# Last feed-forward stage: DMA transposes, two PSUM accumulator sets, a padded bias product and five steps in place of six

## The reference

```python
x = x + 0.5 * ffn(layernorm(x), weight, bias)
x = x + attention(layernorm(x), ...)
x = x + 0.5 * ffn(layernorm(x), weight, bias)      # the last stage

def ffn(x, weight, bias):
    # blocks of 32 channels: scale = max(|block|) / 7.5, values to the nearest of the FP6 grid
    xq, xs = mx_quantize(x)
    wq, ws = mx_quantize(weight)
    return (xq * xs) @ (wq * ws).T + bias
```

## Time and profile before

| what | value |
|---|---|
| median of 3 runs | 3375.26 us (3371.84 to 3376.33) |
| profiled execution: time | 3373.88 us |
| profiled execution: span of the trace | 3372.0 us |
| start of the last stage (its first load) | 2865.46 us |
| busy share over the span: PE, DVE, ACT, POOL | 89%, 68%, 56%, 57% |

### The profile page before, as it was taken

How to read it: one execution, slowest core, us unless ns; L and a number is a source line. 1 busy time by engine, 2 the same in 40 slices (tenths; PEclk the granted TensorE clock), 3 DMA queues, 4 the chain that set the end, 5 groups by cost and what they waited for, 6 DMA issues and landing times. The chain is left out here.

```text
span 3372.0 us, 68516 instructions
## 1 busy us (share of the span) xinstructions
PE 3001.5 (89%) x24864; PEld 1829.5 (54%) x24864; DVE 2306.3 (68%) x3170; ACT 1888.3 (56%) x2323; POOL 1911.1 (57%) x1497
## 2 busy tenths in 40 slices
PE   0399999999999999999978999999999999499999
PEld 0244444444444444444447877777777776244444
DVE  7467666666666766666556666666666665799995
ACT  2355555555555555556545666665666666566662
POOL 3354554554455455445326666666666665788883
PEclk9699999999999999999978999999999999699999
DMA  2123233323323323332247767677767674344442
GB/s 76 63 88 113 88 113 113 107 93 115 119 92 113 113 94 106 113 113 95 93 127 187 191 189 191 189 185 194 188 181 194 187 192 117 115 151 149 149 148 86
DMA packets 339610, 449.44 MB, mean 133 GB/s; under 512 B 23048, under 2 KB 254496, under 8 KB 331168
## 3 DMA queue, kind: packets, MB, share of 16 engines
q1 hardware_dynamic: 339360, 445.57, 43.4%
HBM read 243.85 MB, written 201.38 MB: 132 GB/s over the span
## 5 line engine op out<-in xcount | busy, mean ns | idle before, releaser
L761 DVE TENSOR_TENSOR fq_out_lo<-fq_val,fq_out_hi 128x512 f16<-128x512 f32 x384 | 460.7, 1237 | 289.8 <-ACT fq_out_hi L829 289.8
L946 PE MATMUL fq_acc<-fq_y_hi_t,w_qkv 128*128 128x512 f16 x2048 | 614.6, 379 | 1.6 <-ACT fq_y_hi_t L842 1.6
L1186 ACT ACTIVATE att_ctx<-att_o_ps 32x512 f32<-32x512 f32 x512 | 300.9, 588 | 365.0 <-PE att_o_ps L1295 358.7
L829 ACT CAST fq_out_hi<-fq_val 128x512 f16<-128x512 f32 x384 | 237.3, 618 | 319.1 <-DVE fq_val L758 311.0
L1270 PE MATMUL att_s_ps<-att_k,att_q_bd 128*128 128x44 f16 x6144 | 388.4, 217 | 26.2 <-DMA att_q_bd<-q_parts 16.9
L1270 PEld LDWEIGHTS att_s_ps<-att_k,att_q_bd 128*128 128x128 f16 x6144 | 382.1, 170 | 27.0 <-issue 26.0
L946 PE MATMUL fq_acc<-fq_y_lo_t,w_qkv 128*128 128x512 f16 x1024 | 388.5, 379 | 0.0
L946 PEld LDWEIGHTS fq_acc<-fq_y_hi_t,w_qkv 128*128 128x128 f16 x2048 | 200.1, 98 | 243.6 <-ACT fq_y_hi_t L842 1.8
L946 PE MATMUL fq_acc<-w_qkv,fq_y_hi_t 128*128 128x512 f16 x1024 | 304.9, 380 | 16.7 <-ACT fq_val L824 16.7
L966 PE MATMUL fq_acc<-w_ffn,fq_f_hi_t 128*128 128x512 f16 x1024 | 310.7, 386 | 1.4 <-DVE fq_f_lo_t L806 1.4
L632 PE MATMUL ffn_acc<-w_ffn,ffn_hi_t 128*128 128x512 f16 x1024 | 306.8, 381 | 4.5 <-DVE ffn_x_ring L518 4.4
(11 more groups left out here) (188 smaller groups left out, 6510.2 us busy)
## 6 DMA issues: line engine op xcount, KB each, us to landing
att_v<-v_parts SPq DMA_DIRECT2D x96, 704.0 KB
att_k<-k_parts SPq DMA_DIRECT2D x64, 524.0 KB, 7.1
fq_x<-in_L_attn_x SPq DMA_DIRECT2D x32, 1024.0 KB, 6.8
x_after_ffn<-fq_x SPq DMA_DIRECT2D x32, 1024.0 KB, 4.3
att_q_bd<-q_parts SPq DMA_DIRECT2D x512, 64.0 KB, 3.8
att_x<-x_after_ffn SPq DMA_DIRECT2D x32, 1024.0 KB, 5.9
x_after_attention<-att_x SPq DMA_DIRECT2D x32, 1024.0 KB, 9.2
ffn_x_ring<-x_after_attention SPq DMA_DIRECT2D x32, 1024.0 KB, 6.3
```

The costliest lines, as they stand in the source:

```text
L761: dve.tensor_tensor(out=out[1][:, b], in0=val[:, b % RING], in1=out[0][:, b], op=ALU.subtract).then_inc(s["out_lo"], 1)
L829: act.copy(out[0][:, b], val[:, b % RING]).then_inc(s["out_hi"], 1)
L946: op = pe.matmul(acc[:, b % RING], w, m, start=(kc == 0 and (a, c) == (0, 0)), stop=(kc == KC - 1 and (a, c) == PARTS[-1]))
L1186: return act.activation(ctx_f[rows, u.u % 2].rearrange("p g (c q) -> p g c q", q=CHUNK), o_ps[rows, :, :, h, :], ACT.Copy, scale=1.0 / P_UP)
```

## The change

The diff, cut to what acts. `LAG_*` are the distances of the pipeline's steps.

```diff
-    k.bias_ffn = keep("bias_ffn", [3, C], BF16)
+    k.bias_ffn = keep("bias_ffn", [P, C], BF16)
-    k.ones = keep("ones", [3, P], BF16)
+    k.ones = keep("ones", [P, P], BF16)
...
+                pool.memset(k.bias_ffn[:], 0.0).then_inc(bias_zero, 1)
...
-    LAG_LN, LAG_Q, LAG_LO, LAG_T, LAG_MM, LAG_OUT = range(1, 7)
+    LAG_LN, LAG_Q, LAG_LO, LAG_MM, LAG_OUT = range(1, 6)
...
-        acc = ctx.enter_context(nc.psum_tensor(tag + "acc", [P, SUB, C], F32))
+        acc = ctx.enter_context(nc.psum_tensor(tag + "acc", [P, 2, SUB, C], F32))
...
+                def turn(u, part, part_t, ready, done):
+                    if u.within(GROUPS):
+                        need(sp, s[ready], u.n + 1)
+                        take(sp, s)
+                        need(sp, s["multiplied"], (u.n - 1) * SUB)
+                        take(sp, s)
+                        sp.dma_start_transpose(part_t[:, u.u].rearrange("p i g n -> p (i g) n"),
+                                               part[:, u.u]).then_inc(done[u.u], 16)
...
                         sp.dma_start(dst_v[:, bass.ds(u.n, 1), :], xr[:, slot(u)]).then_inc(stored[u.u], 16)
+                    turn(t.back(LAG_LO), lo, lo_t, "lo_done", lo_turned)
+                    turn(t.back(LAG_Q), hi, hi_t, "hi_done", hi_turned)
...
-                        dve.tensor_scalar(scale[:, u.u], am[:, u.u], 1.0 / FP6_MAX, 1e-30, ALU.mult,
-                                          ALU.max).then_inc(s["floored"], 1)
-                        need(dve, s["floored"], u.n + 1)
-                        dve.tensor_scalar(scale_up[:, u.u], scale[:, u.u], LN_UP * FP8_UP, None, ALU.mult)
-                        dve.reciprocal(rscale[:, u.u], scale[:, u.u]).then_inc(s["scales"], 1)
-                    u = t.back(LAG_T)
-                    if u.within(GROUPS):
-                        need(dve, s["turned_lo"], u.n + 1)
-                        need(dve, s["multiplied"], (u.n - 1) * SUB)
-                        dve.tensor_copy(lo_t[:, u.u], t_lo[:]).then_inc(s["lo_out"], 1)
+                        dve.tensor_scalar(scale_up[:, u.u], am[:, u.u], SCALE_UP / FP6_MAX, SCALE_UP * 1e-30, ALU.mult,
+                                          ALU.max).then_inc(s["floored"], 1)
+                        need(dve, s["floored"], u.n + 1)
+                        dve.reciprocal(rscale[:, u.u], scale_up[:, u.u]).then_inc(s["scales"], 1)
...
-                        need(act, s["turned_hi"], u.n + 1)
-                        need(act, s["multiplied"], (u.n - 1) * SUB)
-                        act.copy(hi_t[:, u.u], t_hi[:]).then_inc(s["hi_out"], 1)
...
-                            for kc in range(KC):
-                                for i in range(SUB):
-                                    op = pe.transpose(dst[:, kc, i * P:(i + 1) * P],
-                                                      x[:, u.u, i * C + kc * P:i * C + (kc + 1) * P], k.ident[:])
...
-                        need(pe, s["hi_out"], u.n + 1)
-                        need(pe, s["lo_out"], u.n + 1)
+                        need(pe, hi_turned[u.u], 16 * (u.h + 1))
+                        need(pe, lo_turned[u.u], 16 * (u.h + 1))
                         for i in range(SUB):
-                            need(pe, s["summed"], (u.n - 1) * SUB + i + 1)
+                            need(pe, s["summed"], (u.n - 2) * SUB + i + 1)
```

More of the change, by code:

```diff
@@ L463, in ffn_phase @@
         lo = sb("lo", [P, 2, W], F16)
-        hi_t = sb("hi_t", [P, 2, KC, GROUP], F16)
-        lo_t = sb("lo_t", [P, 2, KC, GROUP], F16)
+        hi_t = sb("hi_t", [P, 2, SUB, KC, P], F16)
+        lo_t = sb("lo_t", [P, 2, SUB, KC, P], F16)
         bst = sb("bst", [P, 2, SUB, 6], F32)
@@ L517, in body @@
                             x = xr[:, sub_at(u, i)]
-                            dve.scalar_tensor_tensor(out=x, in0=acc[:, i], scalar=k.D_FFN, in1=x, op0=ALU.mult,
+                            dve.scalar_tensor_tensor(out=x, in0=acc[:, u.u, i], scalar=k.D_FFN, in1=x, op0=ALU.mult,
                                                      op1=ALU.add).then_inc(s["summed"], 1)
@@ L554, in body @@
                                           op=ALU.mult).then_inc(s["dequantised"], 1)
+                    u = t.back(LAG_LN)
+                    if u.within(GROUPS):
+                        need(dve, s["ln_done"], u.n + 1)
+                        dve.tensor_reduce(out=am[:, u.u], in_=blocks(xn[:, u.u]), axis=AX.X, op=ALU.max,
+                                          apply_absolute_value=True).then_inc(s["absmaxed"], 1)
+                        need(dve, s["absmaxed"], u.n + 1)
+                        dve.tensor_scalar(scale_up[:, u.u], am[:, u.u], SCALE_UP / FP6_MAX, SCALE_UP * 1e-30, ALU.mult,
+                                          ALU.max).then_inc(s["floored"], 1)
+                        need(dve, s["floored"], u.n + 1)
+                        dve.reciprocal(rscale[:, u.u], scale_up[:, u.u]).then_inc(s["scales"], 1)
                 run(dve, body)
@@ L578, in body @@
                         take(act, s)
[L579 to L580 removed]
+                        act.activation(q8[:, u.u], xn[:, u.u], ACT.Identity, bias=k.tie[:, 0:1],
+                                       scale=SCALE_UP / FP8_UP, saturate=False).then_inc(s["rounded"], 1)
                         need(act, s["dequantised"], u.n + 1)
[L582 removed]
+                        need(act, hi_turned[u.u], 16 * u.h)
                         act.copy(hi[:, u.u], xd[:, u.u]).then_inc(s["hi_done"], 1)
@@ L612, in body @@
                 def body(t):
[L613 to L618, removed]
-                            for kc in range(KC):
-                                for i in range(SUB):
-                                    op = pe.transpose(dst[:, kc, i * P:(i + 1) * P],
-                                                      x[:, u.u, i * C + kc * P:i * C + (kc + 1) * P], k.ident[:])
-                            op.then_inc(s[done], 1)
                     u = t.back(LAG_MM)
                     if u.within(GROUPS):
-                        need(pe, s["hi_out"], u.n + 1)
-                        need(pe, s["lo_out"], u.n + 1)
+                        need(pe, hi_turned[u.u], 16 * (u.h + 1))
+                        need(pe, lo_turned[u.u], 16 * (u.h + 1))
                         for i in range(SUB):
-                            need(pe, s["summed"], (u.n - 1) * SUB + i + 1)
+                            need(pe, s["summed"], (u.n - 2) * SUB + i + 1)
                             for kc in range(KC):
                                 for a, b in PARTS:
-                                    pe.matmul(acc[:, i], (hi_t, lo_t)[a][:, u.u, kc, i * P:(i + 1) * P],
-                                              k.w_ffn[:, b, kc, :], start=(kc == 0 and (a, b) == (0, 0)), stop=False)
-                            pe.matmul(acc[:, i], k.ones[:], k.bias_ffn[:], start=False,
+                                    pe.matmul(acc[:, u.u, i], (hi_t, lo_t)[a][:, u.u, i, kc, :], k.w_ffn[:, b, kc, :],
+                                              start=(kc == 0 and (a, b) == (0, 0)), stop=False)
+                            pe.matmul(acc[:, u.u, i], k.ones[:], k.bias_ffn[:], start=False,
                                       stop=True).then_inc(s["multiplied"], 1)
```

22 lines of the change are left out of this document (7 added, 15 removed).

## The result

| kernel | median us | runs |
|---|---|---|
| before | 3373.94 | 4 (3371.84 to 3376.33) |
| after | 3423.8 | 4 (3416.52 to 3428.26) |

The changed kernel takes 1.0145 times as long, 95% interval 1.0126 to 1.0165. The forecast was 3410 us, its range 3347 to 3465. The profiled span is 3423.0 us against 3372.0.

A forecast was written before the change was run, and what follows sets the result against it. GpSimd's 13.88 us cycle was taken as the bound, TensorE adding 0.2 us. Start, 28 load-loop periods of 12.1 + S and the end gave 3299.5 + 30 S; with S = 3.7, 3410 us, range 3347 to 3465.

The forecast's parts named there:

- The new loop: SyncE's list: statistics, `xd`, `hi`, its transpose issued, next load, statistics; 12.1 us plus S, period 15.8; chance 0.46.
- S: Time by which a transpose on SyncE holds back the load behind it; taken as 3.7 us, ends 0.9 and 6.2.
- The sum: Whole kernel: start, 28 periods of 12.1 + S, last groups and store; span 3297.6 + 30 S, time 3410 us.
- The upper ends: Highest estimates for S: issue 3.9 us from piece counts; data 3.7 us by packet cost, 6.2 at 84 GB/s.
- The load, 4.76 us: Load piece of the loop in the last stage, priced as a load alone, 4.76 us.
- the break-even: Value of S at which the changed kernel takes as long as before: 2.5 us.
- the fast rival: SyncE's list: transposes are quick, S below 2.25, kernel faster; 3351 us at S = 0.9; chance 0.33.
- GpSimd's cycle is 13.88 us long already: Last stage before the change: GpSimd's divisions start 13.88 us apart at the stage's start, with no gap but semaphores.
- TensorE adds 0.2 us to it: Steady part before the change: TensorE lengthens GpSimd's 13.88 us to 14.07; relieving it brings some 6 us in all.
- the cycle stays 13.88: GpSimd after the change: nothing removed, `xd` still blocks the normaliser for 2.2 us, so 13.88 us remains.
- The shown-by list: Signs for right in the last stage: VectorE's load waits, late load issue, period 15.8, GpSimd gaps, TensorE idleness, short tail.
- the signs for "wrong": No load wait and period 13.9; products waiting for `hi_t` or `lo_t`; or `xd` not blocking GpSimd, period below 13.8.

## Why the prediction was right, and where its terms were off

*The new loop decides.* Right, shown from both sides: with the load taken out of it the stage is 72.6 us shorter, and the wait alone, without transposes, makes the old kernel 3.4% slower. That the time came within 14 us of the forecast is partly luck: two terms were off in opposite directions, S too long by 1.3 us and the load too short by 1.7.

*The sum.* It came out 14 us low for reasons that partly cancel. The span forecast for S = 3.7 was 3297.6 + 111 = 3408.6, and 3423.0 was measured. Group 3 has its statistics at 2903.16 (forecast 2905.3); 28 periods of 16.32 instead of 15.8 add 14.6 us; from the statistics of group 31 at 3360.19 to the end it is 62.8 us (forecast 60.9).

*S, the time a transpose holds back the load.* Taken as 3.7, it is about 2.4 in the loop's steps, by the chain above: 1.8 us of issue and 0.4 to 0.7 us until SyncE issues the load (2.2 in the mean of the stretch). The data cost the load some 0.3 us more. Only in the first groups, where the load is issued right behind the transpose, do the data count: 1.8 us and 1.7 of slower landing make 3.5. The upper ends, built on bytes and packets, described a cost that the loop mostly doesn't have.

*The load, 4.76 us.* This is the term that was mis-sized. I took the first load of the stage, which is alone. The row beside it, the median landing of 6.3, was the right one, for in this stage a store is issued within 2 us of the load, in the kernel before (0.7 to 1.1 us ahead of it) and after (1.2 to 2.0 us behind it). The run that moved the store and the one that had no transposes show it. With the true pieces, 2.95 (statistics to `xd`) + 2.35 (`xd` to `hi`) + 1.90 + 0.2 + 2.4 + 6.5 (load to statistics) = 16.3 us. So a loop without any S is 13.9 us long, as long as GpSimd's cycle. The period at which the rest of the change (23.7 us, below) is used up is 13.86 + 23.7 / 28 = 14.7, so the break-even was not at S = 2.5 but near 0.8, and the fast rival had less room than its chance of 0.33 said. The plain copies, with 0.47 us of issue and a load in 5.4 us, show what it would have needed.

*"GpSimd's cycle is 13.88 us long already", "TensorE adds 0.2 us to it", "the cycle stays 13.88".* GpSimd is the bound without the loop: one small step less shortens the stage by 10.6 us. The rest is wrong twice over, and that the new period of 13.86 looks like the forecast's 13.88 is luck. First, the 13.88 are read where the steps are written out. In the loop's steps of the kernel before, GpSimd's divisions are 13.94 and 14.20 us apart in turn, for the idle time before a division is 0.24 and 0.49 us there instead of 0.18. So the 14.07 us are GpSimd's own cycle, and nobody adds to them. From 3000 to 3250 us it is busy 218.94 us, and the 31 that are left are gaps between its own operations, in which it waits for no other engine. Second, the cycle did not stay: with the load ahead it is 13.67 us in the written-out steps and 13.86 in the loop's, 0.21 less in both. What shrank is the block by `xd`. In the kernel before, it starts beside the third small operation, and that one is blocked; now it starts during the low part, and the first small one is blocked until it ends (stretch 3000 to 3250; count, then busy us, mean ns; before, then with the load ahead, where the line numbers are two higher):

```profile
L433 POOL TENSOR_SCALAR ffn_stat<-ffn_mv 128x4 f32<-128x4 f32 x17 | 4.8, 282 | 1.4
L435 POOL TENSOR_TENSOR ffn_stat<-ffn_stat 128x4 f32<-128x4 f32 x18 | 41.5, 2304 | 3.2 <-POOL ffn_stat L434 3.2
```

```profile
L435 POOL TENSOR_SCALAR ffn_stat<-ffn_mv 128x4 f32<-128x4 f32 x19 | 40.8, 2149 | 1.6
L437 POOL TENSOR_TENSOR ffn_stat<-ffn_stat 128x4 f32<-128x4 f32 x18 | 3.6, 198 | 3.2 <-POOL ffn_stat L436 3.2
```

Together 2.59 us before and 2.35 after. VectorE, 98% busy before, was not full either. One of its operations, the scale of 128 x 64 values, is recorded with 2.36 us and the same operation of the changed kernel (L557) with 0.20; before, it starts during GpSimd's low part (3106.78 to 3110.86, say) and ends with it (3108.43 to 3110.92):

```profile
L537 DVE TENSOR_SCALAR ffn_scale<-ffn_am 128x64 f32<-128x64 f32 x18 | 42.5, 2360 | 0.6
```

All this is read from traces; no run changes the block alone.

*What the rest of the change brings.* Predicted 6 us in the steady part and a shorter tail; measured, with the loop taken away, 23.7 us: 6 of period, 19.5 of tail (18.9 us from last low part to last sum against 38.4), less 2 at the start. The 6 of period are right in number, but by the paragraph above they come from the smaller block and not from TensorE. The padded product alone gave the old kernel's stage 1.1 us, and the second accumulator set gave 0.2, neither to be told from nothing.

*The shown-by list.* Wait for the load "nearly 5 us": 5.5. Period 15.8: 16.33. Gaps before GpSimd's normaliser: 1.3 to 3.5 us, 2.6 in the mean. TensorE idle over 4 us: 61.3 us in 15.3 groups, 4.0, so just not over it; some was taken back by the clock (below). Last low part to last sum under 20: 19.7. One of the signs for "wrong" also came true: the products wait for `lo_t`, 57.0 us in 15 waits. It was a bad sign. The transpose lands in 4.2 us, well within the bounds, and TensorE, which has time to spare, waits for whatever comes last: with the load ahead, where the loop is gone, it still waits 33.8 us for `lo_t`.

*The two rules.* A transpose took 4.2 us from issue to landing, all sixteen blocks of it, with 1.8 to 2.3 us of that in the issue; a copy of the same size took 2.9 and 0.47. The Trainium skill, Advanced Engine Details and Errata, section X-Bar Transpose (TRN2), has transposes as fast as regular transfers: these runs disagree. The 21 us in series, my estimate from the 1309 ns for one block in the Trainium skill, VectorE: DVE Perf Modes, section The three transpose paths, are not seen either: sixteen blocks landed in 4.2 us.

## What to carry to other kernels

When DMA issues move to a queue that already carries the loads, write down what each one waits for, and ask whether the load behind it now closes a loop through the engines; then shift the load ahead of it by one step. In such a loop price a transfer by its median in the steady stage, with what is issued beside it, not by one that runs alone. An engine can have plenty of idle time, and each microsecond of its work can still be a microsecond of period, if it stands in the loop.

## What the runs showed of the hardware

**The clock after short idle stretches.** TensorE waits up to 5.8 us for `lo_t`, and behind such a wait its granted clock is at the lower level (windows of the changed kernel, columns as in the earlier trace rows):

```profile
3115.00:3118.00 3.00, 0.00 (x0) 0.00 (x0) 2.82 (x9) 0.00 (x0) 0.31 (x2) 0.78 0.71 183
3118.00:3121.00 3.00, 1.03 (x3) 0.43 (x4) 3.00 (x2) 0.85 (x1) 2.82 (x2) 0.50 0.44 82
3121.00:3124.00 3.00, 3.00 (x9) 1.08 (x8) 2.93 (x5) 1.05 (x1) 1.65 (x8) 0.58 0.18 35
3124.00:3127.00 3.00, 3.00 (x16) 1.36 (x14) 1.60 (x3) 2.93 (x4) 3.00 (x1) 1.00 1.11 200
```

Idle from 3114.3, it starts at 3119.97 at 0.50 (1.2 of 2.4 GHz) and is back at full clock before 3124. In that time two products take 1.03 us, at full clock 0.59. The mean over the stretch is 0.90. I had given it 1 or 2 us in the tail; TensorE is busy 188.66 / 15.3 = 12.3 us a group instead of 4 x 2.81 = 11.2, so it costs 1.1 us a group in the mean, and TensorE still stands idle for 4.0.

**A product with 3 rows costs more than one with 128.** Subtiles are 2.81 us apart with the padded bias product and 3.01 with 3 rows, in an otherwise equal kernel, though both are recorded as 0.38 us.

**A load and a store beside each other.** With the load first and the store 1.4 us behind, the load lands in 6.4 us and the store in 7.7 (6.7 and 8.4 without any transposes, 0.7 us apart); with the store over 5 us ahead they land in 5.1 and 4.5. It is not even-handed: in the kernel before, where the store is issued 0.7 to 1.1 us ahead of the load, the store lands in 4.5 us all the same, and only the load is slow, 6.3.

**VectorE and GpSimd block each other, and the record hides it as busy time.** `xd` takes 2.28 us in the changed kernel and 3.85 with the load ahead, where it starts during GpSimd's low part; the scale above takes 0.20 us or 2.36. A share of 98% can hold 2.2 us a group of such waiting.
